# Attention with three score buffers of each kind, joined maxima and split waits; scan exponents made on GpSimd

## The reference, cut to what matters

```python
x = x + attention(layernorm(x))        # 16 heads of 32, 2 batches of 1024 tokens, causal
x = x + mixture_of_experts(layernorm(x))   # 32 experts, top 8
x = x + state_space(layernorm(x))      # 16 heads, states of 64, chunks of 64
x = x + lut_ffn(layernorm(x))          # weights looked up in a table of 16

# attention, per head
probs = softmax(causal(q @ k.T * scale)); y = probs @ v
# state space, per chunk: cs is the running sum of log decays
L = where(tri, exp(cs[i] - cs[j]), 0)
y = ((C @ B.T) * L) @ X + (C * exp(cs)) @ S_prev
S = exp(cs[-1]) * S_prev + (exp(cs[-1] - cs) * B).T @ X
```

## Time and profile before

| | us |
|---|---|
| median of 3 runs (lowest, highest) | 2613.94 (2613.39, 2614.68) |
| profiled execution | 2616.59 |
| its span, first to last instruction | 2615.0 |
| granted TensorE clock, mean of the span | 0.948 |
| TensorE busy | 2371.0 (91%) |
| VectorE, ScalarE, GpSimd busy | 1570.2, 981.1, 949.5 |
| attention heads, from 171 to 638 | 467 |
| scan, from 1902 to 2200 | 298 |

### The profile page before, as it was taken

One profiled execution on the slowest core, in us unless ns is written; L12 is line 12 of the kernel. 1 busy time (PEld: TensorE's weight loads), 2 busy tenths in 40 slices (PEclk: granted clock), 3 DMA queues, 4 the chain that ended last, 5 costly groups with the idle time before them and its releaser, 6 DMA issues. The chain is left out here.

```text
span 2615.0 us, 48312 instructions
## 1 busy us (share of the span) xinstructions
PE 2371.0 (91%) x12839; PEld 1796.2 (69%) x12840; DVE 1570.2 (60%) x3411; ACT 981.1 (38%) x2202; POOL 949.5 (36%) x862
## 2 busy tenths in 40 slices
PE   7969999996856999999999679999979999899998
PEld 5855555553635988888888558888855554788886
DVE  6435566663665555555555357999178786655554
ACT  3114555553253444444444352222255453311111
POOL 3128888884003666666667311111111110000000
PEclk9978999998866999999999889999999999999999
DMA  5459999995355999999999644457498650100001
GB/s 179 127 174 322 342 348 331 353 327 182 119 207 139 262 275 282 256 256 269 270 250 213 111 142 139 169 170 220 141 257 195 144 147 13 36 25 24 24 9 65
DMA packets 263315, 491.25 MB, mean 188 GB/s; under 512 B 31890, under 2 KB 149138, under 8 KB 253459
## 3 DMA queue, kind: packets, MB, share of 16 engines
q1 hardware_dynamic: 197202, 272.17, 34.3%
q0 software_dynamic: 62976, 212.42, 29.0%
q10 hardware_dynamic: 3024, 5.29, 0.6%
HBM read 592.96 MB, written 198.79 MB: 303 GB/s over the span
## 5 line engine op out<-in xcount | busy, mean ns | idle before, releaser
L1422 PE MATMUL m_ps_u<-m_ring,m_xT_hi 128*128 x1280 | 371.1, 351 | 0.5 <-issue 0.5
L1388 POOL DMA_INDIRECT expert_sum<-x_res,token_of x160 | 256.5, 1603 | 196.2 <-DMA expert_sum<-x_res,token_of 58.7
L798 ACT ACTIVATE probs<-ps_c 128x512 f32<-128x512 f32 (+3 forms) x384 | 182.8, 490 | 214.0 <-PE ps_c L731 130.5
L828 DVE TENSOR_REDUCE neg_max<-ps_r 128x1 f32<-128x512 f32 (+3 forms) x256 | 147.6, 589 | 161.7 <-PE ps_r L698 112.5
L1422 PEld LDWEIGHTS m_ps_u<-m_ring,m_xT_hi 128*128 128x128 f32 x1280 | 237.0, 190 | 1.3 <-issue 0.9
L1422 PE MATMUL m_ps_u<-m_ring,m_xT_lo 128*128 x640 | 217.3, 340 | 0.0
L1381 POOL DMA_INDIRECT m_xg<-x_rows,token_of x160 | 174.2, 1089 | 100.6 <-issue 90.8
L698 PE MATMUL ps_r<-k_st,q_st 96*128 96x512 f32 (+3 forms) x384 | 164.1, 434 | 45.5 <-DVEq L821 18.5
L1860 PE MATMUL s_ps<-s_x_hi,s_w_hi 128*128 128x512 f32 x512 | 199.6, 390 | 1.7 <-POOL s_w_lo L1830 1.7
L1860 PE MATMUL s_ps<-s_x_lo,s_w_hi 128*128 128x512 f32 x512 | 199.2, 389 | 0.0
L1860 PE MATMUL s_ps<-s_x_hi,s_w_lo 128*128 128x512 f32 x512 | 199.2, 389 | 0.0
(11 more groups left out here) (353 smaller groups left out, 5691.0 us busy)
## 6 DMA issues: line engine op xcount, KB each, us to landing
m_ring<-w_split SPq DMA_DIRECT2D x160, 1536.0 KB
m_ring<-w_split SPq DMA_DIRECT2D x160, 768.0 KB
w_split<-e_gu_parts POOLq DMA_DIRECT2D x32, 1536.0 KB
proj<-s_out SPq DMA_DIRECT2D x32, 1024.0 KB, 3.9
e_raw_gu<-w_experts POOLq DMA_DIRECT2D x32, 768.0 KB
w_split<-e_dn_parts POOLq DMA_DIRECT2D x32, 768.0 KB
e_raw_dn<-w_experts POOLq DMA_DIRECT2D x32, 512.0 KB
q_st<-q_parts SPq DMA_DIRECT2D x32, 256.0 KB
```

The costliest lines, as they stand in the source:

```text
L798: nc.scalar.activation(probs[a][j % RING][:, :width], ps_c[a][:, :width], ACT.Exp, scale=SCALE).then_inc(exp_done, 1)
L828: nc.vector.tensor_reduce(dst, ps_r[n % 2][:, :w], AX.X, ALU.max, negate=True).then_inc(max_done, 1)
L1388: pool.indirect_dma_start(acc[j % 2], rows_at(j), y[j % TURNS], None, bounds_check=PADDED - 1, oob_is_err=True, compute_op=ALU.add).then_i ...
L1422: last = nc.tensor.matmul(ps_u[b % 2][:, :W_UP], x[b % 2][:, k, :], ring[:, first + k * GU_ROW:][:, bass.ds(place, W_UP)], start=(n == 0), ...
```

## The change

Attention heads:

- `UPPER` is ordered by key half: all 8 products of upper queries with lower keys, then all 8 with upper keys. The upper queries and the upper keys have a semaphore each, and the keys' is waited for at the first of the last 8.
- `ps_r` and `ps_c` have three banks each; `ps_c` is no longer one per batch but goes round. `probs` has a ring of four. To make room, `ps_turned` and `ps_y` have one bank each.
- `max_cols` holds the parts of both batches for a query block side by side, in columns 96 to 99. Turning takes 4 matmuls. All 32 spare rows are copied into `q_st` for both batches as before, and the spare rows of `k_st` hold ones in rows 96 and 97 for one batch and in 98 and 99 for the other. GpSimd makes these patterns with two selections over 128x1024 and one more fill.
- With one bank of outputs, the copy of each half must be done before the next half's products: VectorE's order has it after maxima 2 and 10 in place of 6 and 12.

Scan: `weigh` goes. GpSimd makes the differences of all four sequences in one subtraction and adds the mask in a second instruction, in each step after its copy. TensorE's order within a step, but for a group's first, has the output projection first.

```diff
-    UPPER = [(a, tb, c, min(HALF, (tb + 1) * P - c)) for a in range(BATCH) for tb in reversed(range(HB, TB)) for c in range(0, T, HALF)]
+    UPPER = [(a, tb, c, min(HALF, (tb + 1) * P - c)) for c in range(0, T, HALF) for a in range(BATCH) for tb in reversed(range(HB, TB))]
+    N_Q_UP = N_LOW + BATCH * HB
-    RING = 3
+    RING = 4
+    BUFS = 3
-        max_cols = sb("max_cols", [P, BATCH, HB, P], F32R)
+        max_cols = sb("max_cols", [P, HB, P], F32R)
-        ps_r, ps_c = [pb(f"ps_r{b}", HALF) for b in range(2)], [pb(f"ps_c{a}", HALF) for a in range(BATCH)]
-        ps_t, ps_y = pb("ps_turned", T), pb("ps_y", T)
+        ps_r, ps_c = [pb(f"ps_r{b}", HALF) for b in range(BUFS)], [pb(f"ps_c{b}", HALF) for b in range(BUFS)]
+        ps_t, ps_y = pb("ps_turned", HALF), pb("ps_y", HALF)
...
+            pool.memset(raw_gu[1][:, :T], 1.0).then_inc(consts, 1)
+            pool.wait_ge(consts, 6 + E)
+            pool.affine_select(out=y_st[:, :], in_=y_st[:, :], compare_op=ALU.is_ge, fill=0.0,
+                               base=K_QK + 1, pattern=[[0, T]], channel_multiplier=-1).then_inc(consts, 1)
+            pool.affine_select(out=raw_gu[1][:, :T], in_=raw_gu[1][:, :T], compare_op=ALU.is_ge, fill=0.0,
+                               base=-K_QK - 2, pattern=[[0, T]], channel_multiplier=1).then_inc(consts, 1)
...
-                        load_q(it + 1, e, 1, up_loaded[e])
-                        load_k(it + 1, e, 1, up_loaded[e])
+                        load_q(it + 1, e, 1, q_up_loaded[e])
+                        load_k(it + 1, e, 1, k_up_loaded[e])
...
                 if n == N_LOW:
-                    pe.wait_ge(up_loaded[e], (it + 1) * 64)
+                    pe.wait_ge(q_up_loaded[e], (it + 1) * 32)
+                if n == N_Q_UP:
+                    pe.wait_ge(k_up_loaded[e], (it + 1) * 32)
...
-                for a in range(BATCH):
-                    for t in range(HB):
-                        last = nc.tensor.matmul(ps_t[:, a * HALF + t * P:a * HALF + (t + 1) * P], max_cols[:, a, t, :], ident_r[:, :], start=True, stop=True)
+                for t in range(HB):
+                    last = nc.tensor.matmul(ps_t[:, t * P:(t + 1) * P], max_cols[:, t, :], ident_r[:, :], start=True, stop=True)
...
-                    nc.vector.tensor_copy(k_st[b][K_QK:, a, :], y_st[K_QK:, :]).then_inc(consts, 1)
+                    nc.vector.tensor_copy(k_st[b][K_QK:, a, :], (y_st[K_QK:, :], raw_gu[1][K_QK:, :T])[a]).then_inc(consts, 1)
...
+                of_batch = max_cols[:, :, K_QK:K_QK + 2 * BATCH].rearrange("p t (a two) -> p a t two", two=2)
-                nc.vector.tensor_copy(max_cols[:, :, :, K_QK], blocks).then_inc(parts_done, 1)
+                nc.vector.tensor_copy(of_batch[:, :, :, 0], blocks).then_inc(parts_done, 1)
...
-                nc.vector.tensor_copy(y_st[:, toks], ps_y[:, toks]).then_inc(y_done, 1)
+                nc.vector.tensor_copy(y_st[:, toks], ps_y[:, :]).then_inc(y_done, 1)
...
-                        maxima(*after(it, e), 0, 6)
+                        maxima(*after(it, e), 0, 2)
                     if not (first and e == 0):
                         evacuate(*before(it, e), 1)
                     if more:
-                        maxima(*after(it, e), 6, N_LOW)
+                        maxima(*after(it, e), 2, N_LOW)
                         parts(*after(it, e), 0)
-                        maxima(*after(it, e), N_LOW, 12)
+                        maxima(*after(it, e), N_LOW, 10)
                     evacuate(it, e, 0)
...
# scan, GpSimd, after the copy into bx_now
+                        if k == 0:
+                            pool.wait_ge(cs_loaded[b], it * 16 + 16)
+                        pool.wait_ge(y_done, n + 1)
+                        cs_chunk = cs_all[b][:, :].rearrange("p (s k i) -> p s k i", s=SEQS, i=P)[:, :, k, :]
+                        own = csT[:, bass.ds((it * 2 + b) * NC, NC)].rearrange("p (s k) -> p s k", s=SEQS)[:, :, k:k + 1]
+                        nc.gpsimd.tensor_tensor(att[k % 2][:, :, :], cs_chunk, own.to_broadcast([P, SEQS, P]), ALU.subtract).then_inc(differences, 1)
+                        pool.wait_ge(differences, n + 1)
+                        nc.gpsimd.tensor_tensor(att[k % 2][:, :, :], att[k % 2][:, :, :], mask[:, :].rearrange("p (o i) -> p o i", o=1).to_broadcast([P, SEQS, P]),
+                                                ALU.add).then_inc(expo_done, 1)
# scan, TensorE
+                        if k > 0 and not (first and b == 0):
+                            project_out(*last_group(it, b), k)
                         if not (final and b == 1 and k == STEPS - 1):
                             prepare(*after(it, b, k))
+                        if k == 0 and not (first and b == 0):
+                            project_out(*last_group(it, b), k)
                         if k < LINKS:
                             new_states(it, b, k)
-                        if not (first and b == 0):
-                            project_out(*last_group(it, b), k)
                         outputs(it, b, k)
# scan, VectorE
-                for s in range(SEQS):
-                    last = nc.vector.scalar_tensor_tensor(att[k % 2][:, s, :], cs_all[b][:, c * P:(c + 1) * P], csT[:, bass.ds(g * NC + c, 1)],
-                                                          mask[:, :], ALU.subtract, ALU.add)
-                        if more:
-                            weigh(*after(it, b, k))
```

More of the change, by code:

```diff
@@ L508, in attend @@
     GU, DN = W_GU, W_RAW - W_GU
-    CONSTS = 12 + 3 * E
+    FROM_POOL = 11 + E
+    CONSTS = FROM_POOL + 4 + 2 * E
     assert len(ROWS) == PER_UNIT and NCH == 12 and N_LOW == 8 and EXPERTS == 2 * HEADS
@@ L675, in _ @@
             for e in range(E):
-                for half, loaded in ((0, low_loaded[e]), (1, up_loaded[e])):
-                    load_q(0, e, half, loaded)
-                    load_k(0, e, half, loaded)
+                load_q(0, e, 0, low_loaded[e])
+                load_k(0, e, 0, low_loaded[e])
+                load_q(0, e, 1, q_up_loaded[e])
+                load_k(0, e, 1, k_up_loaded[e])
             with sp.Fori(0, BODIES - 1) as it:
@@ L728, in columns @@
                 diagonal = t0 == s * P
-                last = nc.tensor.matmul(ps_c[a][:, :width], k_st[e][:, a, s * P:(s + 1) * P], q_st[e][:, a, t0:t0 + width], start=True, stop=not diagonal)
+                last = nc.tensor.matmul(ps[:, :width], k_st[e][:, a, s * P:(s + 1) * P], q_st[e][:, a, t0:t0 + width], start=True, stop=not diagonal)
                 if diagonal:
-                    last = nc.tensor.matmul(ps_c[a][:, :P], ident_bf[:, :], mask_T[:, :], start=False, stop=True)
+                    last = nc.tensor.matmul(ps[:, :P], ident_bf[:, :], mask_T[:, :], start=False, stop=True)
                 last.then_inc(cols_done, 1)
@@ L786, in shift @@
                 for a in range(BATCH):
-                    nc.scalar.copy(q_st[e][K_QK:, a, half * HALF:(half + 1) * HALF], ps_t[K_QK:, a * HALF:(a + 1) * HALF]).then_inc(shift_ready, 1)
+                    nc.scalar.copy(q_st[e][K_QK:, a, half * HALF:(half + 1) * HALF], ps_t[K_QK:, :]).then_inc(shift_ready, 1)
             def body(it, final):
@@ L832, in parts @@
                 blocks = neg_max[:, :, half * HB:(half + 1) * HB]
-                dve.wait_ge(max_done, u * PER_UNIT + (PER_UNIT if half else N_LOW) + 2)
+                of_batch = max_cols[:, :, K_QK:K_QK + 2 * BATCH].rearrange("p t (a two) -> p a t two", two=2)
+                dve.wait_ge(max_done, u * PER_UNIT + (PER_UNIT if half else N_LOW) + BUFS)
                 if half:
@@ L862, in body @@
                     if more:
-                        maxima(*after(it, e), 6, N_LOW)
+                        maxima(*after(it, e), 2, N_LOW)
                         parts(*after(it, e), 0)
-                        maxima(*after(it, e), N_LOW, 12)
+                        maxima(*after(it, e), N_LOW, 10)
                     evacuate(it, e, 0)
                     if more:
-                        maxima(*after(it, e), 12, PER_UNIT)
+                        maxima(*after(it, e), 10, PER_UNIT)
                         parts(*after(it, e), 1)
@@ L2092, in scan @@
             sem(n) for n in ("x_out", "b_out", "att_done", "st_done", "dec_done", "state_done", "y_mm_done", "gated_done", "o_done", "o_added_s")]
+        differences = sem("s_differences")
         block = ctx.enter_context(nc.Block())
```

47 lines of the change are left out of this document (21 added, 26 removed).

## The result

The changed kernel takes 2586.7 us (median of 4 runs, 2584.8 to 2590.1) against 2613.7 for the kernel before, measured beside it: ratio 0.9887, 95% interval 0.9867 to 0.9908, or 27.0 us less. Forecast were 13 us less, in a range of 2590 to 2610. The direction was right; the size was half of it, and 2586.7 lies outside the range.

The account below looks back on a forecast made before the run. TensorE was taken to bound attention and scan, with GpSimd only 16.75 us behind in attention. Attention −14.0 us and scan +1 gave −13, so 2613.94 − 13 = 2601 us, range 2590 to 2610.

Parts of the forecast that it names:

- The step stays 4.70; taking VectorE's work away gains nothing here.: Scan, steady steps: TensorE alone sets the step, so it stays at 4.70 us with less work on VectorE.
- The 6.4 us at the jump stays, less the spare 1.0.: Scan, where VectorE's loop jumps back: its late start stays but for the spare time, −1.2 us in the sum.
- VectorE's jump costs nothing: Rival, scan: VectorE's shorter loop makes its jump back free, 5 us more saved, 2596 us; chance 0.08.
- The first eight steps: Scan, steps without projection: GpSimd's 3.6 us round replaces 4.05, −2 us; first weights come later, +0.9 us.
- At 7 borders: +3.5.: Scan, each group's first step: the score product waits about 0.5 us for the weighting, at 7 borders +3.5 us.
- GpSimd holds VectorE: Rival, scan's steady steps: GpSimd's work delays VectorE's multiplications, 0.47 us in 56 steps, 26 us, 2627 us; chance 0.06.
- The rival of GpSimd's jump: Scan: three jumps of GpSimd's longer loop cost 5 us more, 2606 us, or 16 more, 2617 us; chance 0.12.
- TensorE gains 35 us: Attention: turnings 14.4, upper keys' DMA wait 13 and waits on VectorE's maxima 8 us save TensorE 35 us.
- Of 15.3 us I take 13 away: Attention: awaiting the upper keys eight row products later removes 13 of TensorE's 15.3 us of waits on their DMA.
- Of 25.3 us I take 8: Attention: a third row buffer removes 8 of TensorE's 25.3 us (17.1 + 8.2) of waits on VectorE's maxima.
- so the stage ends at 623.7: Attention: GpSimd's end 620.98, later start 2.2 and leaving 0.5 us give 623.7 against 637.73, −14.0 us.
- the rival of the DMA engines' rate: Attention: DMA engines become the bound; 30 GpSimd stores each 0.3 us late lose 9 us, 2610 us; chance 0.07.

Follow-up runs that it names:

- exponents_only: Kernel before with only the scan's differences moved from VectorE to GpSimd, TensorE's order of products as before; ratio to the kernel before 0.9960.
- order_only: Kernel before with only TensorE's order of the scan step changed (projection first), the differences staying on VectorE; ratio to the kernel before 0.9967.
- longer_list: Changed kernel with 8 one-column memsets added in every step of VectorE's scan loop body; ratio to the kernel before 0.9944.

## Why the prediction was wrong

- **The step that failed is "The step stays 4.70; taking VectorE's work away gains nothing here."** The second half was right (`exponents_only`: 4.70). The first was wrong, because the new order was costed only by what it waits for. The projection was taken at 1.92 us and each group at its own length wherever it stands, while the trace of before already held the 0.76 us in which no weights were loaded. The step is 0.30 us shorter, with the order alone (`order_only`, 4.40) as with the whole change. A group of 8 steps went from 36.64 to 35.3 or 35.4 us, as its border gave 0.5 back, and the first group with a projection took 0.8 longer than before. Apart from the jump and the first steps the scan is 8.1 us shorter.
- **"The 6.4 us at the jump stays, less the spare 1.0."** It went, all 9.0 of it: the forecast took a fixed cost of a jump, where whether it costs anything depends on the length of the loop's list, and it left out the clock behind the wait (2.6 of the 9.0). The rival "VectorE's jump costs nothing" named this, at 5 us more and 0.08: the mechanism was right, the size was off, 1.2 in the sum for 9.0 measured. These two make −17.1 of the scan's −20.6.
- **The first eight steps.** Forecast −2 and +0.9; measured −3.5 together, up to the transposes of step 9; with the 17.1 above that is the scan's −20.6. GpSimd's subtraction with a repeated operand took 1.05 us, less than the 1.27 of the plain one, and the rounds are 3.3 to 3.5 us where 3.6 was forecast. The rival of two far costlier instructions fell.
- **"At 7 borders: +3.5."** The size was right. The two steps of a border take 8.93 us, for 4.32 + 4.12 = 8.44 before: +0.49 each. But the score product waited 0.20 us there, not 0.5, and the projection behind it another 0.38 to 0.48 for VectorE's gate, which the forecast didn't have; so the agreement is in part luck.
- **GpSimd holds VectorE.** It does: the decay of the state (L2351) took 0.51 us in the mean against 0.28, up to 1.06. It reached nobody, as VectorE now waits in each step. The rival of GpSimd's jump fell: its longest pause in the scan that nothing explains is 0.2 us.
- **Attention: "TensorE gains 35 us".** It gained 13.5. The turnings' term was right (0.48 us in the median of 32, for 0.93: 13.9 us). "Of 15.3 us I take 13 away" failed: queries that were issued ahead of the keys are late as well, 5.3 to 21.9 us in the seven profiles of this attention, 12 in the mean, where the keys' wait before is 10.1 to 17.3 in five. "Of 25.3 us I take 8" failed too. The 25.3 added the weight loads' idle time to the products', and during 6.3 of those 17.1 us products ran; the products themselves waited 8.2 us from 200 on, 10.4 in the whole stage. In the seven profiles they wait 13.1 to 25.5. The two waits replace each other: together they are 24 to 27 us in the five stages of before and 30 to 35 in the seven of after. In place of the 21 us that these two terms save, the runs show 7.6 us of waiting added, in the mean.
- **Attention: "so the stage ends at 623.7".** With GpSimd the last, its sum counted. Its start was right (+2.0). "Its heads pass at a steady 26.8 us, without a DMA wait in it" wasn't: the store waits grew by 6.9 us, which is the rival of the DMA engines' rate, priced at 9 and taken with 0.07. And leaving the stage costs 2.8 us, not the estimated 0.5. Of these 9.2 us too much some came back (GpSimd's end without the waits, 449.7, is 2.7 earlier than the 452.4 forecast), and −7.6 was measured for −14.
- **The middle.** "Moves only as a block" holds for its code; its length differs by several us from one execution to the next, which is as much as a term of this sum.

The forecast's bound of −15 for the attention stage has no term behind it: with 2.1 for the start the sum gives −14.1, and what the first load gives back isn't priced.

The sum with the measured terms is −7.6 (attention) and −20.6 (scan), 28.2; the stages of the same code add −0.9 in these two profiles. That the middle's −3.2 and the beginning's +3.5 are chance isn't shown, only that such differences occur without any edit. What stays open is why TensorE loads weights ahead between some shapes and not between others, what sets the cost of the jump (2.65, 9.0 and 11.2 us at lists of nearly one length), and why the wait of 5.3 to 21.9 us on the queries is now on the queries' DMA and now on VectorE's maxima in the same attention code.

## What to carry to other kernels

Where an engine seems full, look at what it does between groups of products: ordering groups so that neighbours have weights of the same shape gave about 0.15 us at each, with no work removed. A jump of a loop with a long body can cost several us (2.7 to 11 here, nothing with the short body), and a long wait that it makes can cost again in TensorE's clock. Where the DMA engines were 0.9 busy, a wait removed on one load came back on the next one or on another engine: TensorE's busy time in the stage fell by 20.4 us, its end moved by 10. And once another engine ends the stage, look at that engine's own waits: a second buffer for GpSimd's store gave 6.8 us more.

## What the hardware did unexpectedly

- GpSimd's subtraction of 128x512 with a repeated operand of one column took 1.05 us, the addition with a repeated row 1.27, as the plain one.
- A selection over 128x1024 on GpSimd took 1.03 to 1.04 us, and a fill of that size 0.95.
- A loop body of 355 instructions (`longer_list`) made VectorE late twice, by 5.0 and 6.9 us, in one pass; one of 226 not at all.
- A pause of 6.39 us on TensorE was followed by a projection at 1.2 GHz (3.78 us for 1.98); a pause of 2.36 us (`order_only`) was not.
- Weights were loaded under running products between 96\*128 and 128\*128, never between 128\*128 and 64\*128, 128\*64 or 128\*33 (trace of the kernel before).
